# Two-layer recurrence: who forms the low half of a state, and what TensorE does before it is there

## The reference

```
def step(carry, gx_t):                 # 126 steps, batch of 16, state h of 256 numbers
    h, c, m = carry
    g = gx_t + h @ Wh                  # gx = x @ Wx + b, g has 5 gates of 256
    i = sigmoid(g[:, 0*H:1*H]); f = sigmoid(g[:, 1*H:2*H])
    c_tilde = tanh(g[:, 2*H:3*H]); o = sigmoid(g[:, 3*H:4*H])
    m_new = tanh(g[:, 4*H:5*H])
    c_new = f * c + i * c_tilde
    h_new = o * tanh(c_new) + m_new
h1 = run_layer(x,  Wx0, Wh0, b0)       # first layer over all steps
h2 = run_layer(h1, Wx1, Wh1, b1)       # second layer reads the first one's states
return h2 @ Wfc + bfc
```

## Time and profile before

| what | value |
|---|---|
| time, median of 3 runs | 1066.12 us (1065.29 to 1070.09) |
| span of the profiled execution, first to last instruction | 1011.2 us |
| lies around the span (1066.12 - 1011.2) | 54.9 us |
| TensorE busy | 857.5 us (85%), 17239 matmuls |
| VectorE busy | 753.3 us (74%) |
| ScalarE busy | 520.8 us (52%) |
| GpSimd busy | 361.6 us (36%) |

### The profile page before, as it was taken

One profiled execution on the slowest core, in us unless ns is written; L12 is line 12 of the kernel. 1 busy time (PEld: TensorE's weight loads), 2 busy tenths in 40 slices (PEclk: granted clock), 3 DMA queues, 4 the chain that ended last, 5 costly groups with the idle time before them and its releaser, 6 DMA issues.

```text
span 1011.2 us, 44652 instructions
## 1 busy us (share of the span) xinstructions
PE 857.5 (85%) x17239; PEld 684.5 (68%) x17239; DVE 753.3 (74%) x3032; ACT 520.8 (52%) x1605; POOL 361.6 (36%) x565
## 2 busy tenths in 40 slices
PE   4666777736899999985799999999999999999595
PEld 2245554513566666662699999999999999976253
DVE  4348897698777676677788888888888888887244
ACT  0535766603666666653355555555555555555073
POOL 0306675565667777750111111111111111100644
PEclk9767998656999999996899999999999999998597
DMA  7710002320122222315200000000000000002133
GB/s 229 277 51 1 1 1 94 129 67 27 42 75 77 77 77 77 77 41 174 86 4 0 0 0 0 0 0 0 0 0 0 0 0 0 0 2 64 42 96 114
DMA packets 30137, 50.64 MB, mean 50 GB/s; under 512 B 7969, under 2 KB 19161, under 8 KB 30074
## 3 DMA queue, kind: packets, MB, share of 16 engines
q1 hardware_dynamic: 23578, 36.95, 11.2%
q0 software_dynamic: 6496, 12.84, 4.7%
HBM read 38.40 MB, written 11.38 MB: 49 GB/s over the span
## 4 chain that ended last, share of the span: by engine, by line
PE 41%; POOL 3%; DVE 3%; issue 2%; DMA 1%; ACT 1%; DVEq 0%; POOLq 0%; SPq 0%
PE quad L1456 20%; PE bank L1456 17%; POOL y_scratch L1759 2%; POOL x_scratch L1753 1%; PE quad L1471 1%; PE bank L1471 1%; DVE post L1616 0%; PE quad L1782 0%; ACT post L1567 0%; PE bank L1444 0%; DVE post L1655 0%; DVE post L1630 0%; DVE post L1624 0%; DVE post L1644 0%; DMA post<-y_scratch 0%
## 5 line engine op out<-in xcount | busy, mean ns | idle before, releaser
L1456 PE MATMUL quad<-post,area 128*128 128x32 f16 (+1 forms) x7520 | 237.4, 182 | 3.2 <-DVE post L1661 2.1
L1456 PEld LDWEIGHTS quad<-post,area 128*128 128x128 f16 x7520 | 217.3, 96 | 17.4 <-DVE post L1661 9.0
L1456 PE MATMUL bank<-post,area 128*128 128x32 f16 (+1 forms) x6260 | 193.4, 180 | 4.7 <-DVE post L1661 2.8
L1456 PEld LDWEIGHTS bank<-post,area 128*128 128x128 f16 x6260 | 176.0, 96 | 17.8 <-DVE post L1661 3.4
L1409 POOL COPY post<-post 128x32 f32 (+1 forms) x126 | 28.6, 227 | 341.6 <-DVE post L1661 341.6
L1553 ACT ACTIVATE post<-post 128x96 f32<-128x96 f32 x252 | 71.4, 283 | 130.9 <-DVE post L1616 130.9
L1616 DVE TENSOR_REDUCE post<-quad 128x96 f32<-128x192 f32 x378 | 99.7, 264 | 3.0 <-PE quad L1456 2.6
L1616 DVE TENSOR_REDUCE post<-bank 128x96 f32<-128x192 f32 x378 | 99.3, 263 | 3.1 <-PE bank L1456 1.5
L885 POOL DMA_INDIRECT y_scratch<-area x78 | 76.9, 986 | 43.0 <-DVE area L1272 23.8
L1567 ACT ACTIVATE post<-post 128x32 f32<-128x32 f32 x252 | 57.8, 229 | 64.5 <-DVE post L1630 64.5
L880 POOL DMA_INDIRECT area<-x_scratch,area x78 | 78.3, 1003 | 28.3 <-issue 21.3
(11 more groups left out here) (328 smaller groups left out, 1756.5 us busy)
## 6 DMA issues: line engine op xcount, KB each, us to landing
w0s<-in_w SPq DMA_DIRECT2D x12, 768.0 KB
area<-in_rec SPq DMA_DIRECT2D x7, 640.0 KB
post<-y_scratch SPq DMA_DIRECT2D x8, 504.0 KB
area<-in_w SPq DMA_DIRECT2D x4, 768.0 KB
area<-in_f SPq DMA_DIRECT2D x2, 1024.0 KB, 7.4
area<-in_patches SPq DMA_DIRECT2D x1, 1488.4 KB
x_scratch<-post SPq DMA_DIRECT2D x1, 1472.0 KB, 7.2
area<-in_taps SPq DMA_DIRECT2D x1, 1350.0 KB
```

The costliest lines, as they stand in the source:

```text
L1456: mm = pe.matmul(at[0][:, at[1] + out.start:at[1] + out.stop], rec_w[:, w, s, m * P:(m + 1) * P], operand, start=False, stop=False, skip_g ...
```

## The change

Three things change in the recurrence.

1. Products of a low weight part take only the high half of a state or input. The product low times low is gone. The own products are reordered: for IFC all twelve low-weight products (16 columns each) come first and wait only for the new semaphore `high0` or `high1`, which VectorE raises when the high half is written. Then TensorE waits for `state0` or `state1`, and the twelve high-weight products (32 columns) follow. OM is low weights, then high weights. For input products of two steps a low-weight product has 2x16 columns instead of 64.
2. VectorE's list is reordered. `new_state` of the other layer moves behind the x sum of this layer (before, it stood in front of it). The two y sums become one of four blocks (128x64). `store_low` leaves VectorE.
3. GpSimd does `store_low`: it waits for `high`, then for the full state (`part`), subtracts, and raises `state`. Its history copy now stands behind `store_low(0, ...)` of the same turn.

The core of the diff:

```diff
@@ rec_pool
+            def store_low(l, n, u):
+                pool.wait_ge(sg(f"high{l}"), n)
+                pool.wait_ge(sg(f"part{l}"), n * 3)
+                settle(pool)
+                pool.tensor_tensor(pair_of(l, u)[:, :, 1, :], hfull[:, l, u, :].rearrange("p (k b) -> p k b", k=KH),
+                                   pair_of(l, u)[:, :, 0, :], ALU.subtract).then_inc(sg(f"state{l}"), 1)
             def both(t, u):
+                if here(t, BEHIND + 1, SEQ + BEHIND):
+                    store_low(1, t - BEHIND, (u - 1) % 4)
                 if u % PAIR == 0 and here(t, 0, SEQ - 4):
                     load(t + PAIR, 1 - u // PAIR)
+                if here(t, 0, SEQ - 1):
+                    store_low(0, t + 1, u)
                 if here(t, BEHIND + 1, SEQ + BEHIND):
                     v = (u - 1) % 4
-                    pool.wait_ge(sg("state1"), t - BEHIND)
                     settle(pool)
                     pool.tensor_copy(...)
@@ rec_pe
+            def high_weights(l, q, w, operand, first, which):
+                for m in which:
+                    mm = pe.matmul(chunk_at(l, q, m, first, operand.shape[1]), rec_w[:, w, 0, m * P:(m + 1) * P], operand,
+                                   start=False, stop=False, skip_group_check=True)
+                return mm
+            def low_weights(l, q, w, operand, first, which):
+                for m in which:
+                    mm = pe.matmul(chunk_at(l, q, m, first, operand.shape[1])[:, :, 0, :],
+                                   rec_w[:, w, 1, m * P:(m + 1) * P], operand[:, :, 0, :],
+                                   start=False, stop=False, skip_group_check=True)
+                return mm
-            def own(l, t, u, states):
-                out = slice(u % PAIR * 32, u % PAIR * 32 + 32)
-                for which, name in ((IFC, "pre_x"), (OM, "pre_y")):
-                    for k in range(KH):
-                        mm = chunks(l, u // PAIR, (WH0, WH1)[l] + k, states[k], out, which)
-                    mm.then_inc(sg(f"{name}{l}"), 1)
+            def own(l, n, u, states):
+                q, odd, w = u // PAIR, u % PAIR, (WH0, WH1)[l]
+                pe.wait_ge(sg(f"high{l}"), n)
+                for k in range(KH):
+                    low_weights(l, q, w + k, states[k], odd, IFC)
+                pe.wait_ge(sg(f"state{l}"), n)
+                for k in range(KH):
+                    mm = high_weights(l, q, w + k, states[k], odd, IFC)
+                mm.then_inc(sg(f"pre_x{l}"), 1)
+                for k in range(KH):
+                    low_weights(l, q, w + k, states[k], odd, OM)
+                for k in range(KH):
+                    mm = high_weights(l, q, w + k, states[k], odd, OM)
+                mm.then_inc(sg(f"pre_y{l}"), 1)
@@ rec_dve, store_state: the high half raises its own semaphore
+                dve.scalar_tensor_tensor(out=high, in0=mem, scalar=H_SCALE, in1=scaled, op0=ALU.mult, op1=ALU.add
+                                         ).then_inc(sg(f"high{l}"), 1)
@@ rec_dve, both
-                if ending:
-                    new_state(1, n1 - 1, v)
                 if first_layer:
                     sum_part(0, n0, u, "x")
                 if ending:
+                    new_state(1, n1 - 1, v)
                     store_state(1, n1 - 1, v)
                 if first_layer:
-                    sum_part(0, n0, u, "y", 0, KH)
-                if ending:
-                    store_low(1, n1 - 1, v)
+                    sum_part(0, n0, u, "y")
...
                 if first_layer:
                     products(0, n0)
                     new_cell(0, n0)
-                    sum_part(0, n0, u, "y", KH, KH)
-                    new_state(0, n0, u)
                 if second_layer:
                     sum_part(1, n1, u, "x")
                 if first_layer:
+                    new_state(0, n0, u)
                     store_state(0, n0, u)
                 if second_layer:
-                    sum_part(1, n1, u, "y", 0, KH)
-                if first_layer:
-                    store_low(0, n0, u)
+                    sum_part(1, n1, u, "y")
...
                 if second_layer:
                     products(1, n1)
                     new_cell(1, n1)
-                    sum_part(1, n1, u, "y", KH, KH)
```

More of the change, by code:

```diff
@@ L1507, in both @@
                 if here(t, 1, SEQ - 1):
-                    pe.wait_ge(sg("state0"), t)
                     before = (u - 1) % 4
-                    own(0, t, u, [hpair0[:, before // PAIR, k, before % PAIR] for k in range(KH)])
+                    own(0, t, u, [hpair0[:, before // PAIR, k, before % PAIR:before % PAIR + 1] for k in range(KH)])
                 if here(t, 0, SEQ - 3):
```

46 lines of the change are left out of this document (20 added, 26 removed).

## The result

The changed kernel takes 1176.04 us (median of 4 runs, 1174.92 to 1177.27); the kernel before, run beside it, takes 1065.84 us (4 runs, 1065.29 to 1070.09). The ratio is 1.1009, with a 95% interval of 1.0979 to 1.104: 110 us slower. The prediction said slower, at 1085 us and at most 1102. The direction was right; the size was short by a factor of more than five, and a mechanism that the prediction priced at nothing carries most of it.

What follows compares the result with a forecast made beforehand. The bound was taken to be a closed ring of waits through both layers. Growth of 0.095 us over 244 halves (+23), single-layer turns (-1) and loop ends (-3) gave +19 on 1066.12: 1085 us, range 1058 to 1102.

Steps and rivals of the forecast that it cites:

- What I cost at nothing: List of side effects in the recurrence priced at zero: TensorE's other work, VectorE's y sum, GpSimd's history copy and load.
- The slack of 0.26: On TensorE, other products are over 2.24 us after the high half, the next restart is at 2.50.
- The ring and its three legs: Closed wait loop through both layers between neighbouring x sums, one half; predicted to grow from 1.655 to 1.755 us.
- (a): VectorE, one layer's x sum to the other's high half; 0.28 us becomes 0.51, with new_state adding 0.23.
- (c): TensorE, own products to that layer's x sum; 0.805 us becomes 0.505 with twelve of 24 products out of the way.
- Leg (b): High half to TensorE's own products, through GpSimd's subtraction of 0.265 us; 0.57 us becomes 0.74.
- The loop's end: VectorE's branch at the end of four turns now falls into a wait; 29 ends at 0.1, -3 us.
- Low half soon there: Rival: full state's end to TensorE's restart takes 0.33 us instead of 0.46, giving 1053 us; chance 0.09.
- TensorE bound: Rival: TensorE limits the recurrence, so only narrower products count, -7 us, 1059 us; chance 0.06.
- Clock falls: Rival: fewer streamed columns drop TensorE's granted clock to 0.50, half 1.91 us, +62, 1128 us; chance 0.07.
- Port lock whole: Rival: GpSimd's subtraction waits until VectorE's products operation ends, +0.20 us a half, 1134 us; chance 0.04.
- The upper bound of 1103: Time if GpSimd's subtraction starts after 0.17 us and takes 0.29; each half then grows by 0.155 us.

Runs made afterwards that it cites:

- e1: The changed kernel with GpSimd's load put ahead of store_low(1); 1089.16 us against 1060.01 for the kernel before, ratio 1.0272.
- e6: The kernel before with only GpSimd's load moved behind the history copy that waits for the second layer's state; 1163.66 us against 1060.01, ratio 1.098.
- e10: The changed kernel, load still late, with TensorE's second-layer products ahead of the bias and input products that wait for the load; 1117.33 us against 1067.76, ratio 1.0485.
- e5: The kernel before with only each new_state moved behind the other layer's x sum; 1112.78 us against 1060.01, ratio 1.0508.
- e4: The kernel before with low-weight products taking only the high half, old waits and places kept; 1061.57 us against 1060.01, ratio 1.0002.
- e0: The kernel before, unchanged, run once more with its profile; 1015.52 us, span 1013.7.
- e3: The kernel before with TensorE's part of the change alone, low-weight products first behind a wait for the high half; 997.43 us against 1012.54, ratio 0.9854.
- e2: The changed kernel with the load ahead of store_low(1) and both new_state back ahead of the other x sum; 1007.49 us against 1012.54, ratio 0.9944.
- e7: The kernel before with only the low half moved to GpSimd, behind the load; 1041.85 us against 1012.54, ratio 1.0291.
- e8: The e3 kernel with eight turns in a round of the loop instead of four; 1076.03 us, ratio 1.0123 to the kernel before.

## Why the prediction was wrong

**The step that failed** is the last sentence of "What I cost at nothing": "GpSimd's history copy and load sit between two subtractions 1.7 us apart and take about 0.4 and 0.9." It asks whether GpSimd has room, and it has. It does not ask who waits for the load. With the load in front of `store_low(1)`, its wait is for nothing of this turn; behind it, it starts after the second layer's state, TensorE's input products wait for it, and the second layer's own products are queued behind those. The slack of 0.26 in front of that sentence has the same fault: it adds up the input products as if their inputs were always there. This was worth 80 us of 108 (e1), and 100 alone on the old kernel (e6); e10 shows that most of it passes through the queue behind the input products. None of the prediction's signs of being wrong looked at the load.

**The ring and its three legs: right in kind, short by a third.** Without the late load (e1) the change costs +28 of recurrence against the +19 forecast. Legs (a) and (c) came within 0.02. Leg (b) was 0.78 instead of 0.74: the subtraction took 0.31 instead of 0.265, and everything else in it was met. The half grew by 0.128 (from 1.652, ends of the loop left out, to 1.780) instead of by 0.095: 244 x 0.033 = 8 of the 9 us.

**`new_state` in the ring: right,** with +52 measured by itself (e5) against 244 x 0.23 = 56. **The loop's end: right;** e1's turn is 3.560, twice its half of 1.780, where the old turn was 0.02 to 0.03 longer than two halves.

**Low weights hidden, narrower products worth nothing: right** in e1 and e4.

**The rivals.** Low half soon there: wrong; the path from the full state's end to the restart was the 0.78 of leg (b) less the 0.28 up to that end, 0.50 (e1), and 0.38 was needed. TensorE bound: wrong (e4). Clock falls: it did fall, to a mean of 0.74 between 560 and 900 us, but not for the reason given: fewer columns alone keep 1.00 (e4), the changed products without the late load keep 1.00 (e1), and the late load with all columns brings 0.86 (e6). It came with the stop of 1.35 us every two turns, and adds some 10 us to it. Port lock whole: wrong; the operations beside each other cost 0.06 to 0.08, as the section at the end shows.

**Two sums** are off without moving the forecast. The upper bound of 1103 leaves out the 3 us of the loop's end; with them it is 1100. And 28 products at 27 ns are 0.76, not 0.80, which puts the clock rival at 1119, not 1128.

**The base.** "With 54.9 around it" was a misreading: 2 us lie around a span (e0), and the rest was the difference between an execution of the quicker kind and runs of the other, 46 us of it in the places that e0 and e4 show. It did not move the forecast, since the change touches only the recurrence.

**And in the experiments** I repeated the fault once: e3 and e2 were forecast by shortening the ring that I knew, at 0.96 and 0.98, without asking for the next ring, which lay 0.1 behind. In e7 and e8 the size and the direction were missed, as said there.

What the whole comes to, in us of recurrence: 415.4 before; TensorE's part alone -16.4 (e3); low half on GpSimd with the y sums whole +10.5 (e2); `new_state` behind the x sum +33.8 (e1); the load behind `store_low(1)` +80.2 (after, 523.5). These prices hold for this order of steps: on the old kernel the low half on GpSimd alone costs 29.5 (e7), and `new_state` alone 52 (e5).

## What to carry to other kernels

When work is put in front of something in an in-order queue, ask of everything behind it not whether the engine has time, but what it now waits for and who is queued behind its consumer: here one waiting subtraction in front of a prefetch tied the prefetch to the recurrence that it was to run ahead of, and cost 80 of 1066 us. After shortening a ring, write out the next one before giving the gain; here the second lay 0.1 us behind the first and took more than half of it. A fallen clock in the page beside a new stall need not be the cause: here it came with the stall, and carried some 10 us against the stall's 73.

## What the runs showed of the hardware that was not expected

- **The clock fell with the late load, not with fewer columns.** A stop of 1.35 or 1.4 us every two turns (8.5 us in the changed kernel) brought the granted clock from 1.00 to 0.74 (after) or 0.86 (e6) over 560 to 900 us; halved columns did not move it (e4). The time that TensorE stands in all does not order the runs: e5, busy 304.29 of these 340 us, has 1.00, and e10, busy 314.01 and with no wait over 0.8 us, has 0.86. What decides is not shown.
- **GpSimd beside VectorE costs tens of ns on one of the two.** With the start of both at 701.26 (e1) the subtraction takes 0.31 and `products` 0.22; with `products` 0.03 later (e7) it is 0.24 and 0.30. `new_cell` beside a copy takes 0.25 instead of 0.19 (e3). The Trainium skill's page "SBUF — State Buffer", section "SBUF: two separate sides", has the later one blocked fully when VectorE's operation has two SBUF inputs. None of these three places agrees: the operations overlap, and none shows more than 0.08 for 32 and 64 elements a partition.
- **A longer loop body can bring stops of microseconds.** With eight turns a round TensorE stood up to 4.7 us with no engine to wait for, at the end of about every second round, while 0.79 MB of instructions were moved in 280 us (e8); with four turns it has no such stops and no such transfers (e3). That the one causes the other is likely, not shown.
- **One kernel, two times.** Unchanged, its medians are 1012.54 and 1015.83 us in two sets of runs and 1060.01 and 1067.76 in two others. The recurrence takes 415.3 to 415.4 us in profiles of the first kind and 415.2 in e4, of the second; the difference lies in the stages that gather rows by DMA, ahead of the recurrence and behind it.
